# One fused decoder layer on one core: the attention's value product in 512-column matmuls, seven exchange blocks on GpSimd, weight blocks at other pairs

## The reference, cut to what matters

```python
C_q = Q @ Wq_d                       # 4 x 512 x 128
C_kv = K @ Wkv_d                     # 4 x 1601 x 64: the latent of keys and values
CqWqk = (C_q @ W_qk).reshape(b, n, H, LKV)          # 16 heads of 64
scores = jnp.einsum('bnhl,bkl->bhnk', CqWqk, C_kv) / sqrt(LKV)
attn = softmax(scores, axis=-1)
V_up = (C_kv @ Wv_u).reshape(b, nkv, H, HD)
out = jnp.einsum('bhnk,bkhd->bnhd', attn, V_up)
```

## Time and profile before

| | |
|---|---|
| time, median of 3 runs | 2739.88 us (2732.51 to 2740.12) |
| the profiled execution | 2740.16 us, span of its instructions 2738.2 us |
| granted TensorE clock, mean of the span | 0.988 |
| PE busy in the span | 2602.3 us (95%) |
| DVE, ACT, POOL busy | 2315.4 (85%), 1670.2 (61%), 1966.1 us (72%) |
| attention: first and last score product start | 323.1 and 1403.3 us |
| feed-forward network: first work of PE | 1430.2 us |

### The profile page before, as it was taken

How to read it: one execution, slowest core, us unless ns; L and a number is a source line. 1 busy time by engine, 2 the same in 40 slices (tenths; PEclk the granted TensorE clock), 3 DMA queues, 4 the chain that set the end, 5 groups by cost and what they waited for, 6 DMA issues and landing times.

```text
span 2738.2 us, 42011 instructions
## 1 busy us (share of the span) xinstructions
PE 2602.3 (95%) x14328; PEld 1979.5 (72%) x14328; DVE 2315.4 (85%) x2664; ACT 1670.2 (61%) x2619; POOL 1966.1 (72%) x1473
## 2 busy tenths in 40 slices
PE   7998899999999999999988999999999999999997
PEld 4665666666666666666656888888888888788885
DVE  2766688989998999899857999899998899899988
ACT  3444687877787778787855445454455555555553
POOL 1002377677777778777857999999887888888883
PEclk9899999999999999999999999999999999999999
DMA  7426677687778776877681222112223222132221
GB/s 276 157 100 206 212 236 216 188 240 206 223 214 261 206 219 204 259 228 221 201 278 69 100 93 93 70 70 70 77 70 123 77 85 78 70 116 79 83 93 77
DMA packets 166792, 420.64 MB, mean 154 GB/s; under 512 B 30130, under 2 KB 57652, under 8 KB 166068
## 3 DMA queue, kind: packets, MB, share of 16 engines
q1 hardware_dynamic: 164276, 409.57, 47.2%
q10 hardware_dynamic: 2304, 8.39, 0.8%
HBM read 248.43 MB, written 75.04 MB: 118 GB/s over the span
## 4 chain that ended last, share of the span: by engine, by line
PE 44%; SPq 3%; DVE 2%; POOL 1%; issue 1%; ACT 1%; DMA 1%; POOLq 0%; ACTq 0%; DVEq 0%
PE c_ps L1610 42%; SPq L912 2%; PE c_ps L1622 1%; DVE c_sum_g L1766 0%; DVE c_stats L1826 0%; DMA c_ident<-in_ident 0%; POOL b_rw L1357 0%; PE c_ps L1631 0%; POOL c_sum_g L1851 0%; PE b_po L1038 0%; PE b_sc L1019 0%; DVE c_acc L1766 0%; DMA b_rz<-in_c_dz 0%; DMA b_rz<-in_c_gz 0%; ACT c_sg L1674 0%
## 5 line engine op out<-in xcount | busy, mean ns | idle before, releaser
L1766 DVE SCALAR_TENSOR_TENSOR c_acc<-c_ps,c_sd,c_acc 128x1024 f32<-128x1024 f32 x440 | 562.9, 1282 | 90.8 <-PE c_ps L1610 90.7
L1668 ACT ACTIVATE c_scaled<-c_ps,c_sgu 128x1024 f32<-128x1024 f32 x336 | 375.2, 1117 | 422.5 <-PE c_ps L1610 414.7
L1101 ACT ACTIVATE b_pr<-b_sc,b_nm 128x799 f32<-128x799 f32 (+1 forms) x512 | 477.7, 935 | 169.4 <-DVE b_pr L1190 146.9
L1851 POOL TENSOR_TENSOR c_sum_u<-c_sum_u,c_scaled 128x1024 f32<-128x1024 f32 x168 | 404.8, 2410 | 99.6 <-ACT c_scaled L1668 98.3
L1851 POOL TENSOR_TENSOR c_sum_g<-c_sum_g,c_scaled 128x1024 f32<-128x1024 f32 x168 | 405.1, 2411 | 73.2 <-ACT c_scaled L1668 72.2
L1019 PE MATMUL b_sc<-b_kh,b_qs 128*128 128x402 f32 (+1 forms) x1024 | 398.6, 389 | 45.0 <-ACT b_pr L1101 41.2
L1197 DVE STREAM_TRANSPOSE b_tn<-b_pr 128x1280 f32<-128x1280 f32 x256 | 385.4, 1506 | 28.7 <-ACT b_pr L1101 14.6
L1315 POOL COPY b_pt<-b_tn 32x640 f32<-32x640 f32 x430 | 307.4, 715 | 141.7 <-DVE b_tn L1197 82.5
L1019 PE MATMUL b_sc<-b_kl,b_qs 128*128 128x402 f32 (+1 forms) x1024 | 355.9, 348 | 0.0
L1766 DVE SCALAR_TENSOR_TENSOR c_sum_g<-c_ps,c_sgu,c_sum_g 128x1024 f32<-128x1024 f32 x224 | 286.4, 1278 | 26.0 <-PE c_ps L1610 20.6
L1190 DVE TENSOR_SCALAR_CACHE_REDUCE b_pr<-b_sc,b_nm_first 128x799 f32<-128x799 f32 x256 | 268.7, 1050 | 29.1 <-PE b_sc L1019 8.3
(11 more groups left out here) (212 smaller groups left out, 4871.0 us busy)
## 6 DMA issues: line engine op xcount, KB each, us to landing
b_pt<-b_tn SPq DMA_DIRECT2D x774, 80.0 KB, 2.7
shared<-b_tn SPq DMA_DIRECT2D x378, 80.0 KB, 2.8
c_uw_int<-wint_u SPq DMA_DIRECT2D x56, 512.0 KB, 3.5
c_gw_int<-wint_g SPq DMA_DIRECT2D x56, 512.0 KB, 3.4
c_dw_int<-wint_d SPq DMA_DIRECT2D x56, 512.0 KB, 3.4
a_cx<-in_b_ctxT SPq DMA_DIRECT2D x16, 1608.0 KB, 9.8
b_rw<-in_c_gw SPq DMA_DIRECT2D x28, 512.0 KB, 4.1
b_rz<-in_c_gz SPq DMA_DIRECT2D x28, 512.0 KB, 5.6
```

The costliest lines, as they stand in the source:

```text
L1101: S.activation(pr[u % 2][:, k0:k1], sc[:, at + lo:at + hi], ACT.Exp, bias=nm[:, u % 2:u % 2 + 1], accum_out=den[:, g % 2, q, half:half + 1 ...
L1668: S.activation(dst[:, :], pair[SLOT[x, t] % 4][:, :], ACT.Identity, scale=scale(x, t)).then_inc(s_e, 1)
L1766: V.scalar_tensor_tensor(out=total, in0=pair[SLOT[x, t] % 4][:, :], scalar=scale(x, t), in1=before, op0=ALU.mult, op1=ALU.add).then_inc(s_ ...
L1851: G.tensor_tensor(total, total, scaled[m % 2][:, :], ALU.add).then_inc(s_add, 1)
```

## The change

`weigh` works on a head (512 moving columns, 4 units) and is spread over four steps: three tiles from `pe`, then 4, 3 and 3 tiles from `pt`. `pt` and `pe` become two buffers of a head each in place of three of a pair. `cross` goes: its two blocks join POOL's list. `FREE` is spaced evenly up to pair 26. The feed-forward network loads one weight block less ahead of time and its SBUF tiles stand in another order; several semaphores are merged (the same events, counted in one).

```diff
-BY_POOL = [(0, 0), (1, 1), (2, 2), (3, 3), (0, 1)]
-BY_SCALAR = [(3, 2), (2, 3)]
+BY_POOL = [(0, 0), (1, 1), (2, 2), (3, 3), (0, 1), (3, 2), (2, 3)]
...
-FREE = (2, 5, 8, 11, 14, 20, 21, 22, 23, 30, 31)
+FREE = (2, 5, 8, 11, 14, 17, 20, 23, 26, 30, 31)
...
-WEIGH_AT = 6
-LATENT_AT = 9
+WEIGH_AT = 7
+WEIGH_PARTS = [(10, 11, 12), (0, 1, 2, 3), (4, 5, 6), (7, 8, 9)]
+LATENT_AT = 10
...
-            def weigh(p, part):
-                b, s, g = p // 2 // HEADS, p % 2, p // 2
+            def weigh(g, part):
+                b = g // HEADS
                 if part == 0:
-                    moved(T, p)
-                    T.wait_ge(s_pe, 2 * p + 2)
-                    if s == 0 and g:
+                    T.wait_ge(s_pe, UNITS * (g + 1))
+                    if g:
                         T.wait_ge(s_ot, g)
...
-                for t in (range(0, 7), range(7, NKT))[part]:
-                    z = t % 2
+                elif part == 1:
+                    moved(T, 2 * g)
+                    moved(T, 2 * g + 1)
+                for n, t in enumerate(WEIGH_PARTS[part], sum(len(x) for x in WEIGH_PARTS[:part])):
+                    z = n % 2
                     if t < NDT:
-                        turned = pt[p % MOVES][:, :, :, 32 * t:32 * t + 32].rearrange("p a z e -> p z a e")
+                        turned = pt[g % 2][:, :, :, 32 * t:32 * t + 32].rearrange("p a u e -> p u a e")
                     else:
-                        turned = pe[p % 3][:, t - NDT, :, :]
-                    ins = T.matmul(po[z * LAT:(z + 1) * LAT, s * 256:(s + 1) * 256], cn[:, b, t, :], turned,
-                                   start=(t < 2), stop=(t >= NKT - 2))
+                        turned = pe[g % 2][:, t - NDT, :, :]
+                    ins = T.matmul(po[z * LAT:(z + 1) * LAT, :], cn[:, b, t, :], turned,
+                                   start=(n < 2), stop=(n >= NKT - 2))
...
-            def cross(p):
-                s = p % 2
-                S.wait_ge(s_tt, 2 * p + 2)
-                if p >= MOVES:
-                    S.wait_ge(s_pv, p - MOVES + 1)
-                for a, c in BY_SCALAR:
-                    S.copy(pt[p % MOVES][32 * c:32 * c + 32, a, :, :], tn[s][32 * a:32 * a + 32, c, :, :]).then_inc(s_cross, 1)
```

More of the change, by code:

```diff
@@ L166, in sync @@
             for dst, src in ((wd, d["wd"]), (bd, d["bd"])):
[L167 removed]
+                Q.dma_start(dst[:], src).then_inc(xin[0], 16)
             for z in range(2):
@@ L409, in scalar @@
                     S.wait_ge(small, 10 * 16)
[L410 to L413, removed]
+                    S.wait_ge(s_prep, 3)
+                    S.activation(alog[:, :], alog[:, :], ACT.Exp).then_inc(s_soft, 1)
+                    S.activation(g1[:, :], g1[:, :], ACT.Sigmoid).then_inc(s_soft, 1)
+            S.wait_ge(s_prep, 6)
             def keep_context(pair):
@@ L866, in attention @@
         nm0 = sb("b_nm_first", [P, 2])
-        den = sb("b_den", [P, 2, QT, 2])
-        rd = sb("b_rd", [P, 2, QT])
+        small = shared[:, end - 16 * SEG - NB - 32:end - 16 * SEG - NB]
+        den = small[:, 0:16].rearrange("p (a q z) -> p a q z", a=2, q=QT)
+        rd = small[:, 16:24].rearrange("p (a q) -> p a q", a=2)
+        var, step = small[:, 24:28], small[:, 28:32]
         stats = sb("b_stats", [P, QT, 2, 6])
@@ L886, in half_at, with landing, landing_free @@
             return 1024 if half else u % 2 * 2048
+        def landing(p, a, c):
+            z = p % 2 * 2
+            return pt[p // 2 % 2][32 * c:32 * c + 32, a, z:z + 2, :]
+        def landing_free(eng, p):
+            if p >= 4:
+                eng.wait_ge(s_pv, p // 2 - 1)
         def moved(eng, p):
@@ L1465, in ffn @@
         sgu = sb("c_sgu", [P, 2 * KC, NI])
-        part = {n: [sb(f"c_sum_{n}{j}", [P, HALF]) for j in range(2)] for n in "gu"}
-        scaled = [sb(f"c_scaled{j}", [P, HALF]) for j in range(2)]
         sg = sb("c_sg", [P, HALF])
-        h = sb("c_h", [P, HALF])
         stats = sb("c_stats", [P, OR, 2, 6])
@@ L1472, in ffn @@
         rstd = sb("c_rstd", [P, OR])
-        d1 = sb("c_dw_int1", [P, HID], F32R)
-        w = {"g": [sb("c_gw_int0", [P, HID], F32R)], "u": [sb("c_uw_int0", [P, HID], F32R)]}
-        for n in "gu":
+        h = sb("c_h", [P, HALF])
+        w = {n: [sb(f"c_{n}w_int0", [P, HID], F32R)] for n in "ug"}
+        part = {n: [sb(f"c_sum_{n}{j}", [P, HALF]) for j in range(2)] for n in "gu"}
+        scaled = [sb(f"c_scaled{j}", [P, HALF]) for j in range(2)]
+        for n in "ug":
             w[n].append(sb(f"c_{n}w_int1", [P, HID], F32R))
-        w["d"] = [sb("c_dw_int0", [P, HID], F32R), d1]
+        w["d"] = [sb(f"c_dw_int{j}", [P, HID], F32R) for j in range(2)]
         xs = sb("c_xs", [P, XR, HID])
```

110 lines of the change are left out of this document (53 added, 57 removed).

## The result

The changed kernel took 2772.1 us (median of 4 runs, 2765.22 to 2775.27), the kernel before 2740.0 beside it (4 runs, 2732.51 to 2745.27). The ratio is 1.0116, 95% interval 1.0097 to 1.0135: about 32 us, where 27 were predicted. In the profiled execution the attention, from the first to the last maximum of DVE, takes 1112.7 us; before it was 1077.7 (the same two instructions, 326.14 to 1403.85). What follows the last maximum takes 1335.5 us after and 1334.3 before, so the loss lies in the attention.

What follows compares the result with a forecast made beforehand. PE was taken as the attention's bound, fullest at 1031.9 of 1078 us; 54 - 26 + 7 - 8 = +27 us on 2740.16 gave 2767 us, 1.0% slower, range 2744 to 2805.

Steps and rivals of the forecast that it cites:

- The value product, +54 us of PE: Attention on PE: tiles without a partner pay whole 512-column slots, so a head costs 0.84 us more, 54 over 64 heads.
- a fixed cost per matmul: Rival, value product on PE: half as many matmuls save a fixed cost, 41 us less, 2726 us; chance 0.03.
- the overlapped odd tile: Rival, value product: PE runs a lone tile beside the next step's first products; 2722 us; chance 0.04.
- ACT's two copies, -26 us: Steady groups: removing ACT's copies, with the longer steps, cuts PE's waits by 0.80 us a group, 26 in 32.
- POOL, +7 us: Attention: two further copies make POOL late in pairs 17 to 23, 3 to 4 us in each of three batches; bounds 0 and 40.
- The rival that POOL becomes the bound (+40): Attention: POOL's 1053 us of work is felt in each busy pair, 40 us instead of 7, 2800 us; chance 0.18.
- The spacing, -8 us: Batch ends: evenly spaced weight blocks free pair 26, saving a third of 24 us of idle time; bounds 0 and 24.
- At nothing: Terms counted as zero: merged semaphores, the weight block loaded later, and two buffers for three.

Runs made afterwards that it cites:

- e8: The kernel before with only the weight blocks evenly spaced; 2733.85 us, ratio 0.9970 to the kernel before.
- e2: The changed kernel with two of POOL's seven block copies put back on ACT; 2749.98 us, ratio 1.0034 to the kernel before.
- e3: The changed kernel with each 512-column matmul of the value product split into two of 256; 2770.89 us, ratio 1.0111 to the kernel before.
- e12: e9 with parts of 3, 4, 4 and 2 tiles, the short part in another step; 2751.71 us, ratio 1.0048 to the kernel before.
- e9: The changed kernel with parts of 2, 4, 4 and 3 tiles and two block copies back on ACT; 2717.98 us, ratio 0.9911 to the kernel before.
- e7: The kernel before with only ACT's two block copies moved to POOL; 2760.67 us, ratio 1.0063 to the kernel before.
- e10: The changed kernel with POOL's normalisations cut from 1024 columns to 8; 2762.93 us, ratio 1.0069 to the kernel before.
- e1: The changed kernel with value-product parts of 2, 4, 4 and 3 tiles; 2755.46 us, ratio 1.0036 to the kernel before.
- e4: The changed kernel with the weight blocks back in their old steps; 2773.79 us, ratio 1.0118 to the kernel before.
- e11: The changed kernel with parts of 2, 4, 4, 3 and one block copied by ACT, two in pairs where POOL is late; 2716.98 us, ratio 0.9903.

## Why the prediction was right, and where its parts were not

The direction, the size (27 us predicted, 32 measured) and the group (33.9 predicted, 33.74 measured) were right. Between kernels that differ in one part, the ratios give, each within 3 to 7 us: the spacing alone -8 us (e8); from there to e2, which adds the 512 columns and what else the change has, +17.5 (0.0064); from e2 to the changed kernel, the copies, +22.5 (0.0082). The sum is the 32 us, as it must be along such a chain. The parts of the prediction were +28 for the product and the copies' waits, +7 for POOL and -8.

**The value product, +54 us of PE.** Right as a statement on PE: four parts of 1.87 us where two were of 1.45. PE's busy time rose by 51 us, but some of that is half clock: e2, with the same product, has 1075.41 us in the attention, 43.5 above the kernel before. e3 excludes a fixed cost per matmul of the size that the rival used, and the three tiles at 1.86 exclude the overlapped odd tile. In the sum it stood beside the next term.

**ACT's two copies, -26 us.** This is the step that failed. The waits of 0.98 us in a group did vanish, and 33.02 + 1.68 - 0.98 = 33.72 is the group that was measured. But of the 0.80 us a group I laid 0.38 to ACT's copies and only 0.42 to the longer step, and e2 has the copies and the same group: the longer parts hide the waits by themselves. What decides then is PE's work beside the output; that is argued from three kernels that differ in other ways too, with e12 as its test. Where that part takes 1.45 us (before), 1.87 (changed) and 1.01 (e9), the group takes 33.02, 33.74 and 32.05: two heads in a group, so 0.84 more and 0.88 less on PE there give +0.72 and -0.97. e12 shows the other side, that a slot saved one step earlier is worth nothing. In the kernel before, whose short parts leave the waits open, the copies are worth 0.5 us a group (e7); in the changed kernel, nothing. So their removal can't be priced apart from the parts.

**POOL, +7 us.** The mechanism is the one predicted and stands in the rows: late cast, store, exchange, transpose. The term was mis-sized: 22.5 us (e2). It left out two things. POOL is also late behind the key splits, which the prediction did not count (the transposes two pairs after the pairs 37 and 69 wait 1.0 and 1.2 us for their exchange), and a lateness is carried on: POOL's copies start 3.8 to 7.3 us behind the pair's transpose in the pairs 20 to 26 of the batches after the first, where I had named 17 to 23. It also had no term for TensorE's clock, which fell to half behind PE's waits.

e10 lays some 13 us to the normalisations (5 to 20 by the intervals). The rest is for the smaller part the key splits: between the profiled executions of e2 and of the changed kernel, 2.6 us of the 22.2 lie in the groups behind them (pairs 36 to 47 and 68 to 79), and 19.9 in the pairs 56 to 67, 84 to 99 and 120 to 127, where the normalisations and the batches' ends are. What makes POOL late there beside the normalisations, no kernel here takes away by itself.

The rival that POOL becomes the bound (+40) is not what happened: POOL is busy 998 of 1113 us, 90% and not above 93, 31.41 of 33.74 in a steady group, and the waits for the exchange stand bunched. But 22.5 lies half way between the two prices, and with the shorter groups of e1 POOL costs more, 34 us against e9. Up to 15 of these are the clock's, as an estimate: it stands at 0.5 for 57.6 us of e1's attention and for 27.3 of e9's.

**The spacing, -8 us.** Right for the kernel before (e8), wrong for the changed one: undone there, it makes no difference (e4). I added the terms as though they were independent; but where POOL is late anyhow, moving a block moves the lateness.

**At nothing.** What follows the attention, with the later weight load in it, is 1.2 us longer in the profiled executions; e8, which loads as the kernel before, is there 2.3 us longer, so no cost can be seen. The merged semaphores and the two buffers were not tried by themselves; they stand in e2, e9 and e11 too, which leaves no room for a large cost.

So the total was nearer than its terms: 10 us too much for the product and the copies' waits together, 15 too little for POOL. That these two errors nearly cancel is luck.

## What to carry to other kernels

Before counting an engine's extra work on the path, ask in which step it falls: here 0.84 us of TensorE beside the output set the whole group, and the same 0.84 us one step earlier was free. When a matmul is widened, cut the work so that the parts without a partner fall away, and put the shortest part into the fullest step; with both copies left on ACT that makes this change 0.9911 instead of 1.0116. An engine that fits on average (POOL at 90% of the stage) is late where other work is bunched, and a DMA queue in order passes its lateness on. Count for a long wait of TensorE more than its length: here 3.25 us idle were followed by 6.8 us at half clock.

## What the runs showed of the hardware that was not expected

A matmul of 512 columns and two of 256 cost TensorE the same within about 1 ns each (0.03 us for 26 more, e3), so the width alone buys nothing here. A pair of tiles by itself in a part took 1.01 us (e9), three or four 1.86 to 1.87, so the cost goes in steps of 0.86 and not with the number of tiles.
